# Attention and FFN layer on one core: the probabilities of half 1 are split into high and low parts in two chunks of 2048 columns instead of four of 1024

## What is computed

```python
x = L0_attn_x
x = x + attention(layernorm(x), W_Q, W_K, W_V, W_O)      # causal softmax, scale 1/sqrt(128)
x = x + ffn(layernorm(x), weight, bias, gamma, beta)     # second layernorm, ternary weight, + bias
```

## Time and profile before

| | |
|---|---|
| median of 3 runs | 820.55 us (819.53 to 821.32) |
| the profiled execution | 819.02 us |
| its span, first to last instruction | 816.9 us |
| granted TensorE clock over the span | 1.000 |
| busy: TensorE matmul | 808.9 us, 99% of the span |
| busy: VectorE | 655.7 us, 80% |
| busy: ScalarE | 558.7 us, 68% |
| busy: GpSimd | 547.2 us, 67% |

### The profile page before, as it was taken

The page is one execution under the profiler, slowest core; times in us unless marked ns, Lnnn a source line. Parts: engine busy times, 40 slices in busy tenths (PEclk is TensorE's granted clock), DMA queues, the critical chain, the costliest instruction groups (busy, mean ns, idle before and its releaser), DMA issues.

```text
span 816.9 us, 14674 instructions
## 1 busy us (share of the span) xinstructions
PE 808.9 (99%) x4878; PEld 726.5 (89%) x4878; DVE 655.7 (80%) x1438; ACT 558.7 (68%) x1031; POOL 547.2 (67%) x280
## 2 busy tenths in 40 slices
PE   8999999999999999999999999999999999999998
PEld 7988998888999888998888899888899888899887
DVE  7988787878777878778877878877878787878888
ACT  6877666667676666676766766666766766776684
POOL 6178765686666856768557785569675686585486
PEclk9999999999999999999999999999999999999999
DMA  6456656556556565566654676555766555555603
GB/s 187 95 140 144 171 136 142 117 135 166 138 134 151 134 153 123 139 146 149 161 122 112 152 177 143 127 119 126 175 140 141 130 130 141 128 138 137 150 6 105
DMA packets 57226, 111.50 MB, mean 136 GB/s; under 512 B 16960, under 2 KB 21184, under 8 KB 57152
## 3 DMA queue, kind: packets, MB, share of 16 engines
q1 hardware_dynamic: 57152, 110.56, 56.6%
HBM read 10.88 MB, written 2.10 MB: 16 GB/s over the span
## 4 chain that ended last, share of the span: by engine, by line
PE 95%; DVE 2%; SPq 1%; ACT 1%; DMA 0%; issue 0%; POOL 0%; POOLq 0%; ACTq 0%
PE ring L650 25%; PE scores L688 25%; PE ring L627 21%; PE ring L636 11%; PE ring L659 11%; SPq L445 1%; PE ring L668 1%; PE scores L750 1%; PE ring L591 1%; DMA pT<-turn 0%; DVE acc L861 0%; DVE turn L849 0%; PE ring L601 0%; DVE scores L841 0%; DVE stats L879 0%
## 5 line engine op out<-in xcount | busy, mean ns | idle before, releaser
L521 POOL TENSOR_TENSOR pT<-pT 128x1024 fp32r<-128x1024 f32 x186 | 444.4, 2407 | 256.9 <-ACT pT L786 256.3
L841 DVE CUSTOM_DVE_ANT_0 scores<-scores,mask 128x128 f32<-128x128 f32 (+7 forms) x256 | 194.3, 759 | 148.0 <-PE scores L688 146.3
L779 ACT ACTIVATE turn<-scores,negmax 128x128 f32<-128x128 f32 (+7 forms) x256 | 189.1, 739 | 145.8 <-DVE negmax L841 80.2
L688 PE MATMUL scores<-kT,qT 128*128 128x512 f32 (+3 forms) x1152 | 234.2, 342 | 0.1
L650 PE MATMUL ring<-pT,v 128*128 128x512 f32 x1116 | 217.2, 348 | 0.1
L650 PEld LDWEIGHTS ring<-pT,v 128*128 128x128 f32 x1116 | 187.6, 189 | 28.8 <-issue 0.4
L786 ACT ACTIVATE pT<-pT 128x1024 fp32r<-128x1024 f32 x186 | 195.4, 1057 | 17.0 <-DMA pT<-turn 16.4
L688 PEld LDWEIGHTS scores<-kT,qT 128*128 128x128 f32 x1152 | 186.6, 189 | 19.2 <-ACT turn L779 0.9
L849 DVE STREAM_TRANSPOSE turn<-turn 128x128 f32<-128x128 f32 (+1 forms) x248 | 187.3, 766 | 0.2 <-ACT turn L779 0.2
L659 PE MATMUL ring<-wo_s,zT 128*128 128x256 f32 x768 | 112.0, 282 | 0.2 <-DVE zT L912 0.2
L861 DVE SCALAR_TENSOR_TENSOR acc<-ring,inv,acc 128x256 f32<-128x256 f32 x256 | 109.7, 470 | 0.0
(11 more groups left out here) (79 smaller groups left out, 510.7 us busy)
## 6 DMA issues: line engine op xcount, KB each, us to landing
pT<-turn SPq DMA_DIRECT2D x496, 128.0 KB, 2.3
pT<-turn SPq DMA_DIRECT2D x496, 64.0 KB, 2.0
acc<-in_x SPq DMA_DIRECT2D x8, 256.0 KB, 5.5
wk_raw<-in_wk SPq DMA_DIRECT2D x8, 256.0 KB, 2.9
wq_raw<-in_wq SPq DMA_DIRECT2D x8, 256.0 KB, 3.7
wv_raw<-in_wv SPq DMA_DIRECT2D x8, 256.0 KB, 2.9
norm<-in_wo SPq DMA_DIRECT2D x8, 256.0 KB, 2.9
out<-acc SPq DMA_DIRECT2D x8, 256.0 KB, 2.5
```

The costliest lines, as they stand in the source:

```text
L521: pool.tensor_tensor(chunk(half, LO, c), f32(chunk(half, LO, c)), f32(chunk(half, HI, c)), ALU.subtract).then_inc(plo_ready, 1)
L688: mm = pe.matmul(scores[:, t % 2, first + c:first + c + n], qT[:, par, a, t * P:(t + 1) * P], kT[:, par, m, c:c + n], start=(i == 0), stop ...
L779: act.activation(turned, columns, ACT.Exp, bias=negmax[:, t % 2:t % 2 + 1], scale=-1.0, accum_out=rowsum[:, u % 2, t:t + 1]).then_inc(prob ...
L841: dve.tensor_tensor_reduce(out=tile, in0=tile, in1=mask[:, S - (t + 1) * P:S], scale=-1.0, scalar=FAR, op0=ALU.add, op1=ALU.min, accum_out ...
```

## The change

CHUNKS becomes (2, 2): half 1 has two chunks of two quadrants, 2 x 8 x 128 = 2048 columns each. In the lists the items of half 1's four chunks become two. In SCALAR chunk 0 now stands where chunk 1 stood, behind `("exp", 3, 0)`, and chunk 1 where chunk 3 stood, behind `("exp", 4, 0)`; in the start and the end the items are moved likewise. The wait at L643 follows CHUNKS, and is for the second of two chunks instead of the fourth of four.

```diff
 SCALAR = (
     ("exp", 5, -1), ("pv", 0, -2), ("qk", 3, 0), ("exp", 6, -1), ("exp", 7, -1), ("hip", 0, 0, -1), ("qk", 1, 0),
-    ("pv", 1, -2), ("exp", 0, 0), ("exp", 1, 0), ("qk", 2, 1), ("hip", 0, 1, -1), ("hip", 1, 0, -1), ("exp", 2, 0),
-    ("v", 0, 0), ("exp", 3, 0), ("hip", 1, 1, -1), ("qk", 0, 1), ("v", 1, 0), ("hip", 1, 2, -1), ("exp", 4, 0),
-    ("hip", 1, 3, -1),
+    ("pv", 1, -2), ("exp", 0, 0), ("exp", 1, 0), ("qk", 2, 1), ("hip", 0, 1, -1), ("exp", 2, 0),
+    ("v", 0, 0), ("exp", 3, 0), ("hip", 1, 0, -1), ("qk", 0, 1), ("v", 1, 0), ("exp", 4, 0),
+    ("hip", 1, 1, -1),
 )
 GPSIMD = (
-    ("split", "k", 1), ("split", "v", 0), ("split", "q", 1), ("lop", 0, 0, 0), ("lop", 0, 1, 0), ("lop", 1, 0, 0),
-    ("lop", 1, 1, 0), ("lop", 1, 2, 0), ("lop", 1, 3, 0), ("split", "o", -1),
+    ("split", "k", 1), ("split", "v", 0), ("split", "q", 1), ("lop", 0, 0, 0), ("lop", 0, 1, 0),
+    ("lop", 1, 0, 0), ("lop", 1, 1, 0), ("split", "o", -1),
 )
...
 START_SCALAR
-    ("exp", 1, 1), ("x", 6), ("hip", 0, 1, 0), ("v", 0, 1), ("exp", 2, 1), ("hip", 1, 0, 0), ("hip", 1, 1, 0),
-    ("x", 7), ("exp", 3, 1), ("v", 1, 1), ("qk", 2, 2), ("hip", 1, 2, 0), ("qk", 0, 2), ("exp", 4, 1),
-    ("hip", 1, 3, 0),
+    ("exp", 1, 1), ("x", 6), ("hip", 0, 1, 0), ("v", 0, 1), ("exp", 2, 1), ("hip", 1, 0, 0),
+    ("x", 7), ("exp", 3, 1), ("v", 1, 1), ("qk", 2, 2), ("qk", 0, 2), ("exp", 4, 1),
+    ("hip", 1, 1, 0),
...
 END_SCALAR
-    ("hip", 1, 0, 30), ("pv", 0, 30), ("tp", 1), ("tp", 2), ("hip", 1, 1, 30), ("hip", 1, 2, 30), ("exp", 4, 31),
-    ("exp", 5, 31), ("hip", 1, 3, 30), ("pvl", 0), ("tp", 3), ("tp", 4), ("std2", 0), ("tp", 5), ("exp", 6, 31),
+    ("pv", 0, 30), ("tp", 1), ("tp", 2), ("hip", 1, 0, 30), ("exp", 4, 31),
+    ("exp", 5, 31), ("hip", 1, 1, 30), ("pvl", 0), ("tp", 3), ("tp", 4), ("std2", 0), ("tp", 5), ("exp", 6, 31),
...
-    CHUNKS = (2, 4)
+    CHUNKS = (2, 2)
```

More of the change, by code:

```diff
@@ L97 @@
     ("clear", 1), ("split", "k", -1), ("split", "q", -1), ("split", "v", -1), ("lop", 0, 0, 0), ("lop", 0, 1, 0),
-    ("lop", 1, 0, 0), ("lop", 1, 1, 0), ("lop", 1, 2, 0), ("lop", 1, 3, 0), ("split", "o", -1), ("lop", 0, 0, 1),
-    ("lop", 0, 1, 1), ("lop", 1, 0, 1), ("lop", 1, 1, 1), ("lop", 1, 2, 1), ("lop", 1, 3, 1),
+    ("lop", 1, 0, 0), ("lop", 1, 1, 0), ("split", "o", -1), ("lop", 0, 0, 1),
+    ("lop", 0, 1, 1), ("lop", 1, 0, 1), ("lop", 1, 1, 1),
 )
```

## The result

The changed kernel takes 858.28 us (median of 4 runs, 856.63 to 863.8), against 820.04 us before (median of 4, 818.89 to 821.32): a ratio of 1.0477, 95% interval 1.045 to 1.0504, so 38.2 us slower. The profiled execution took 856.89 us, with a span of 855.1.

A forecast was written before the change was run, and what follows sets the result against it. TensorE was taken as the bound, with the loop feeding pv(1) taking over. Losses of 3.4 + 26.2 + 2.4 + 3.0 = 35.0 us on 819.02 gave 854.0, plus 1.5 for the median: 855.5 us, range 843 to 869.

The forecast's parts named there:

- The loop and its bound: Five-engine loop feeding pv(1), not yet the bound, becomes it: +20 to +50 us, chance 0.84.
- The prices: Instructions of 2048 columns: 1.92 us on ScalarE, 4.65 on GpSimd; loop grows by 3.10 us.
- The slack and SyncE's return: Before pv(1), 1.85 us of slack per unit; SyncE's shorter issue lag gives 0.28 us back.
- The sum per unit: Per steady unit 3.10 - 1.85 - 0.28 = 0.97 us lost; 26.2 us over 27 units.
- The ends: Losses outside the 27 steady units: 3.4 us in units 0 and 1, 2.4 in 29, 3.0 in 30.
- Units 0 and 1: At the start, slack of 1.35 us makes unit 0 about 1.7 late, unit 1 alike: 3.4 us together.
- Unit 30: Near the end, two GpSimd low parts of 4.65 us back to back make pv(1) 3.0 us late.
- Unit 29: Near the end, no slack before pv(1) and 0.7 us back from SyncE's lag: 2.4 us late.
- SyncE as the bound: Rival: waves bound by SyncE's issues, not pv(1), so delay vanishes in its queue; 820.5 us, fully hidden chance 0.03.
- The larger loss: Rival: no return from SyncE's lag and doubled instruction prices; around 870 us, up to 52 us lost, chance 0.05.
- Moved steps: Reordered ScalarE and GpSimd items cost nothing; GpSimd's first low part, done some 6.6 us after starting, clears before the second.
- The clock rival: Waits ahead of pv(1) drop TensorE's clock from 2.4 to 1.2 GHz each unit; 980 us in all, chance 0.02.

The follow-up runs named there:

- e7: Kernel before the change, with five memsets ahead of GpSimd's last low part in units 2 to 27; 819.87 us, ratio 1.0 to before.
- e8: Kernel before the change, with seventeen memsets ahead of GpSimd's last low part in units 2 to 27; 843.12 us, ratio 1.0288 to before.
- e10: Kernel before the change, with only the last two high parts of half 1 merged and low parts kept at 1024 columns; 859.92 us, ratio 1.05.
- e4: Changed kernel, with the last high part ahead of exp 4 instead of behind it in the steady part; 839.75 us, ratio 1.0243 to before.
- e1: Kernel before the change, with only the first two quadrants of half 1 merged (chunks 2048, 1024, 1024); 829.09 us, ratio 1.0111.
- e6: Changed kernel, with the fourth wave of half 1 issued by ScalarE behind exp 2 instead of by SyncE; 857.75 us, ratio 1.0478 to before.
- e11: Half 1 in chunks of 1024, 1024, 2048, its fourth wave issued by ScalarE behind exp 2, against the kernel before; 838.92 us, ratio 1.0229.

## Why the prediction was right

**The loop and its bound.** Right. Forecast 855.5 us, range 843 to 869; measured 858.28. pv(1) waits for its low part in all steady units. e7 and e8 show the slack, e10 that the order of the work counts and not the size of GpSimd's instruction, e4 that what stands in front on ScalarE counts alike. TensorE's wait for GpSimd came out at 22.3 us, where some 30 were forecast. The rest of the longer unit shows as busy time of TensorE: 24.66 us of each 25.42 (642.11 of 662.00 us), 24.36 before; the ends of matmuls are modelled.

**The prices.** 1.92 us was forecast for the high part and 1.91 measured, 4.65 and 4.61 for the low one. The 4497 ns that the Trainium skill has in GPSIMD Engine Reference, section 3.1, for this many columns are not what this kernel shows (4611); the slope between 512 and 1024 columns was closer. Together the growth was 0.85 + 2.20 = 3.05 instead of 3.10.

**The slack and SyncE's return.** 1.85 us held. exp 4 starts 12.92 us after pv(1) instead of 13.15, so 0.23 came back, not 0.28. The lag of the first issue is 0.12 us on average, 0.36 before; it is 0.08 or 0.09 in 25 of the 27 units, and 0.16 and 1.20 in two. It was luck that this miss of 0.05 and the one of 0.05 in the prices cancel.

**The sum per unit.** 0.97 forecast, 1.06 measured. What was missing is 0.09 us of pv(1) itself: with a wait in front its first to last matmul takes 4.98 us, without 4.89. 27 units: 28.6 us instead of 26.2.

**The ends.** Units 0 and 1: 2.9 us instead of 3.4. Unit 30: 2.8 instead of 3.0, by the two low parts in one piece that were forecast:

```profile
813.36 9.13 POOL L521 TENSOR_TENSOR pT<-pT 128x2048 fp32r<-128x2048 f32 x2 [5.71 <-ACT pT L786]
822.46 4.86 POOL L537 TENSOR_SCALAR norm<-acc,mv,rstd 128x256 f32<-128x256 f32 x4
...
822.63 4.98 PE L650 MATMUL ring<-pT,v 128*128 128x512 f32 x24 [2.96 <-POOL pT L521]
```

Unit 29: 4.8 us instead of 2.4, the one term that was clearly off. 1.6 us of this is the clock, below. The rest is SyncE: it was to give 0.7 back, but its lag fell only from 0.77 to 0.56 us, and exp 4 starts 14.22 us after pv(1) instead of 14.01, 0.2 later. The tail gives 0.9 back. Sum: 2.9 + 28.6 + 4.8 + 2.8 - 0.9 = 38.2 us of span (855.1 against 816.9), forecast 35.0.

**The rivals.** SyncE as the bound fell with its first issue in the new loop, at 389.84, which follows the end of pv(1) by 0.08 us, and with e8: its queue takes up 0.2 us of 2.87. The larger loss didn't come. That the first low part is out of the way before the second (in "Moved steps") was right for the changed kernel, but by a microsecond only; e1 and e6 show that path as the next bound. The clock rival came true in one unit, and with it one of the signs of being wrong, a granted clock under 1.0 (0.998 over the span). In unit 29 TensorE stood still 0.98 us for an exponential and 2.19 for the low part, and in 793 to 801 the granted clock is 0.79 on average, so part of it at 1.2 GHz:

```profile
789.88 1.65 PE L688 MATMUL scores<-kT,qT 128*128 128x512 f32 x6 [0.98 <-ACT turn L779]
793.72 6.53 PE L650 MATMUL ring<-pT,v 128*128 128x512 f32 x24 [2.19 <-POOL pT L521]
```

pv(1) took 6.53 us instead of 4.97: 1.6 of the 2.4 us by which this term was short. That the clock stays at 1.00 in the 662 us before, with waits of at most 0.88 us ahead of the steady pv(1), agrees with the forecast. The Trainium skill, TensorE: Matmul & The Clock Gate, "HAM oscillation — how this bites in real kernels", has a kernel whose clock falls back at the wait of every tile; in this trace it didn't at any of the 27 steady waits.

The length of the wait alone doesn't decide. The next pv(1), of unit 30, began after 2.96 us of waiting and ran at full clock (the row at 822.63 above: 4.98 us), and so it did in e11 after 2.45 us. In e1 and e4 the same pv(1) took 6.53 and 6.52 us after waits of 2.93 and 2.96 us. What else counts is open.

## What to carry to other kernels

When several engines hand a buffer around in a loop, merging chunks is judged by the last one: all work behind the last transfer adds to the loop, while the fixed costs saved lie beside the bound. Measure the slack of the loop before the merge (distance from the last producer to its consumer, less a hand-over that has no slack), and expect the price to come back in every turn once the slack is spent. Merge the first chunks rather than the last (9 us lost instead of 37 here), look which queue then ends last (e1), and put the last producer ahead of other work on its engine (e4).

## What was not expected of the hardware

- A wait ahead of a run of 24 matmuls costs 0.09 us more than the wait (4.98 instead of 4.89 us).
- GpSimd's price is nearly per column: one low part of 2048 columns takes 4.61 us, two of 1024 in one piece 4.74.
- With a wave issued by ScalarE beside SyncE's (e11), transfers land later: in 3.9 us (ScalarE's) and 2.5 us (SyncE's) instead of 2.3, and one in 5.35 us in the unit shown.
- The granted clock fell once in the changed kernel, to 0.79 on average over the 8 us around a pv(1) that began after 2.19 us of waiting, 0.98 us of waiting shortly before it. A wait of 2.96 us ahead of the next pv(1) left it at full clock.
